# Attention block with two layer norms: the bias add of the layer-norm stages moves from VectorE to GpSimd

## The chip, the cores and the metric

One Trainium2 chip, all 8 cores running the same program, each on two of the 16 sequences. The metric is the device time of the slowest core in microseconds (us). Below, PE is TensorE, DVE is VectorE, ACT is ScalarE, POOL is GpSimd and SP is SyncE.

## What is computed

Layer 0 of a transformer with post layer norms; x is 16 x 2048 x 1024 in float32.

```python
x = _layernorm(x + attn(x, W_attn, b_attn, W_proj, b_proj))      # 16 heads of 64, causal
x = _layernorm(x + ffn(x, G1_R, G2_R, G1_I, G2_I, b_real, b_imag))

# attn ends with:            y @ W_proj + b_proj
# ffn, halves of the row being real and imaginary part:
out_real = x_real @ W_real.T - x_imag @ W_imag.T + bias_real
out_imag = x_real @ W_imag.T + x_imag @ W_real.T + bias_imag
```

The FFN is one product with a 1024 x 1024 matrix built from W_real and W_imag. So each half of the layer ends alike: a 1024 x 1024 product, plus a bias, plus the residual, then a layer norm over the 1024 columns (no gain, no shift).

## The kernel before

A scheduler class (`Sched`) collects the instructions of each engine in five lists, in the order in which `S.emit(engine, ...)` is called; "pe", "ac", "dv", "po" and "sy" are PE, ACT, DVE, POOL and SP. Each engine runs its list strictly in that order. Waits are semaphore counts: ("dv", v) means that DVE must have completed its v-th counted instruction. POOL's list holds DMA issues as well as arithmetic.

Per sequence (`s_i` is 0, 1) the stages are: load x in 16 tiles of 128 tokens and transpose them on PE (`emit_xload`, `emit_xtp`, `emit_xevac`); the V product; attention by pairs of heads, with the Q and K products of the next pair mixed in; a reload of x into `x_tok` (16 tiles side by side, 128 x 1024 float32 each) by four DMAs issued on POOL (line 713); and then two calls of `linear_ln`:

- the first call (`x1_mode` true, called LN1 here) multiplies the attention output by `Wp_sb`, adds the bias `bp_bc` and `x_tok`, normalises, and leaves the result in `x_tok` (float32) and, transposed by PE, in `yfeat` (bf16);
- the second (LN2) multiplies `yfeat` by `Wbig_sb`, adds `bf_bc` and `x_tok`, normalises in place and stores the rows.

In `linear_ln`, for tile `tt`:

- `stage_a(tt)`: PE does 16 matmuls into `ps_s[tt % 2]`, one of two PSUM buffers, each of which comes free when `t2` has read it. Then `t2a` (line 751) adds the bias row, spread over 128 partitions in bf16, to the tile of `x_tok`. `t2` (line 758) adds the matmul result out of PSUM. `st1`, `st2` (lines 763, 767) and `ag` (line 771) form mean and variance, on DVE. `l1` and `l2` (lines 777, 781) on ACT turn the variance into 1/sqrt by Ln and Exp.
- `stage_b1`, kept as `stageB[tt]`: `nm` (line 787, DVE) forms -mean/sqrt(var). In LN1, `xb` (line 792, ACT) writes the normalised tile in bf16 to `x1stage`, and `xf32` (line 801, POOL) then normalises `x_tok` in place, waiting for `xb`. In LN2 `xf32` (line 809, POOL) waits for `nm`, and SP stores the tile (line 815).
- `stage_b2(tt)`, LN1 only: PE transposes `x1stage` (line 826), ACT copies the result to `yfeat` (line 846).

The order in which the tiles are put into the lists is written in this loop:

```python
            for tt in range(n_tt):
                if x1_mode and tt > 2:
                    stage_b2(tt - 3)
                if tt > 0:
                    stageB[tt - 1]()
                stageB[tt] = stage_a(tt)
```

`n_tt` is 16. With two sequences and two calls `t2a` is emitted 64 times.

Of the kernel before, what the change touches and what calls it, by code (L numbers as in the profile page):

```python
# [51 lines left out]
def build(n_seq=2, n_tt=16):  # L52
# [78 lines left out]
    S = Sched()  # L131
# [25 lines left out]
    def bias_bcast(dst, wait_qb, src_row=None):  # L157
# [4 lines left out]
        for jh in range(2):  # L162
# [7 lines left out]
            def cp(v, jh=jh, dst=dst):  # L170
# [7 lines left out]
                  inc="q_b", amt=16)  # L178
# [3 lines left out]
                  waits=[("q_b", S.val("q_b")), ("pe", v_pe_bv)],  # L182
                  inc="q_b", amt=16)
    v_bpbc, v_pe_bp = bias_bcast(bp_bc, v_qb)
    S.emit("po", lambda g: g.dma_start(out=row_bf[0:1, 0:512], in_=b_real[:]),
           waits=[("q_b", S.val("q_b")), ("pe", v_pe_bp)], inc="q_b", amt=16)
    v_qb = S.emit("po", lambda g: g.dma_start(out=row_bf[0:1, 512:1024],
                                              in_=b_imag[:]),
                  waits=[("q_b", S.val("q_b"))], inc="q_b", amt=16)
# [14 lines left out]
    for fi, wdst in enumerate([w2r_d, w2i_d]):  # L204
        vpe = 0
        for m in range(8):
# [10 lines left out]
            vpe = S.emit("pe", mm, waits=w_list, inc="pe" if m == 7 else None)  # L217
# [6 lines left out]
        for m in range(8):  # L224
            sem = "q_w2" if m % 2 == 0 else "q_w3"
            ring = "sy"
            def stf(g, m=m, fi=fi, wdst=wdst):
# [4 lines left out]
                   inc=sem, amt=16)  # L232
# [4 lines left out]
    for wave in range(2):  # L237
# [3 lines left out]
        for i in range(4):  # L241
# [4 lines left out]
                waits=w_extra, inc="q_wa", amt=16)  # L246
        v_wa_ld = S.val("q_wa")
        for i in range(4):
            cc = wave * 4 + i
            if i % 2 == 0:  # L250
# [3 lines left out]
                    waits=[("q_wa", v_wa_ld)], inc="ac")  # L254
            else:
# [3 lines left out]
                    waits=[("q_wa", v_wa_ld)], inc="dv")  # L259
# [7 lines left out]
        inc="q_bt", amt=16)  # L267
# [7 lines left out]
                   waits=[("q_m", v_id)], inc="dv")  # L275
    v_bqkbf = emit_qm(lambda s: s.dma_start(out=bqk_bf[:], in_=battn_d[:],
                                            transpose=True),
                      waits=[("q_bt", v_battn)])
# [3 lines left out]
                   waits=[("q_m", v_bqkbf)], inc="ac")  # L282
# [32 lines left out]
    for dc in range(CC):  # L315
# [3 lines left out]
            inc="q_w", amt=16)  # L319
# [5 lines left out]
    for s_i in range(n_seq):  # L325
# [5 lines left out]
        def sbc(name, shape, dtype):  # L331
# [9 lines left out]
            waits=[G["x_tok"], G["v_all"], ("ac", v_wa_ac), ("dv", v_wa_dv),  # L341
                   ("pe", v_setup_pe)],
            inc="dv")
# [163 lines left out]
        for hp in range(NPAIR):  # L507
# [170 lines left out]
            def yst_store(s, s_i=s_i, hp=hp, yst_=ystage[par]):  # L678
# [4 lines left out]
                         inc="q_ys%d" % par, amt=16)  # L683
            G["yst%d" % par] = ("q_ys%d" % par, vys)
            ys_val.append(vys)
            if hp >= 6:
                v_xf_free = S.val("pe")
                for hp2 in (range(7) if hp == 6 else [7]):
# [5 lines left out]
                           waits=[("q_ys%d" % (hp2 % 2), ys_val[hp2]),  # L694
                                  ("pe", v_xf_free)],
                           inc="q_yf", amt=16)
# [10 lines left out]
        for q4 in range(n_tt // ntq):  # L707
            def xt(s, s_i=s_i, q4=q4, ntq=ntq, x_tok=x_tok):
# [9 lines left out]
                   inc="q_xt", amt=16)  # L718
        v_xt = S.val("q_xt")

        def linear_ln(win_sb, w_wait, feat_ready_fn, bias_bc, v_bias, x1_mode,
# [3 lines left out]
            def stage_a(tt):  # L725
                feat_ready = feat_ready_fn(tt)
                reg = ps_s[tt % 2]
                vpe = 0
                for dc in range(CC):
                    for jh in range(2):  # L730
# [8 lines left out]
                        if dc == 0 and jh == 0:  # L739
                            w_list.append(G["ps_s%d" % (tt % 2)])  # L740
                        r = S.emit("pe", mm, waits=w_list,
                                   inc="pe" if (dc == CC - 1 and jh == 1) else None)
                        if r:
                            vpe = r
# [4 lines left out]
                def t2a(v, tt=tt, x_tok=x_tok, bias_bc=bias_bc):  # L749
                    xt_ = x_tok[:, tt * 1024:(tt + 1) * 1024]  # L750
                    return v.tensor_tensor(xt_, xt_, bias_bc[:], ALU.add)  # L751
                v_t2a = S.emit("dv", t2a,
                               waits=[("q_xt", v_xt), ("dv", v_bbc),
                                      ("po", v_po_base), G["x_tok"]],
                               inc="dv")
                def t2(v, tt=tt, par=par, x_tok=x_tok, reg=reg):
                    xt_ = x_tok[:, tt * 1024:(tt + 1) * 1024]
                    return v.tensor_tensor(xt_, xt_, reg, ALU.add)  # L758
                v_t2 = S.emit("dv", t2, waits=[("pe", vpe), ("dv", v_t2a)],
                              inc="dv")  # L760
                G["ps_s%d" % par] = ("dv", v_t2)
                def st1(v, tt=tt, x_tok=x_tok, stt=stt):
# [7 lines left out]
                def ag(v, mv=mv, stt=stt):  # L770
                    return v.bn_aggr(mv[:, 0:2], stt[:])  # L771
                vag = S.emit("dv", ag,
                             waits=[("dv", vs2), ("ac", ln_guard[sl]["ac"]),
                                    ("dv", ln_guard[sl]["dv"]),
                                    ("po", ln_guard[sl].get("po", 0))], inc="dv")
# [73 lines left out]
# [6 lines that stand above are left out]
# [88 lines left out]
```

How the kernel before makes its waits and increments, by code:

```python
    def run(self, eng_name, engine, sems):  # L40
        floors = {}
        for waits, fn, inc, amt in self.ops[eng_name]:
            for s, v in waits:
                if v and v > floors.get(s, 0):
                    engine.wait_ge(sems[s], v)
                    floors[s] = v
            instr = fn(engine)
            if inc is not None:
                instr.then_inc(sems[inc], amt)
# [850 lines left out]
            @block.sync  # L900
            def _(s):
                S.run("sy", s, sems)
                s.wait_ge(sems["q_out"], v_out_final)
```

## Time and profile before

| | |
|---|---|
| time, median of 3 runs | 1643.38 us (1639.96 to 1705.62) |
| profiled execution: time / span of its slowest core (core 6) | 1641.53 / 1640.0 us |
| spans of the 8 cores | 1617.6 to 1640.0 us |
| busy PE / DVE / ACT / POOL | 1099.8 / 579.2 / 704.6 / 139.8 us |
| DVE `t2a`, both biases | 64 times, 77.8 us |
| POOL `xf32`, LN1 / LN2 | 38.2 / 63.2 us, 32 times each |

Times within the profile are microseconds from the start of the span. A busy share is an average over stages that differ; the timeline lists the instructions of all engines by their start, and is the view in which an order of waits can be followed. Where the rows below are of the timeline, each begins with start and duration, and the brackets at its end give the idle time of that engine before it and what ended that. Runs of like instructions are merged (x16), their duration being that from the first to the last.

### The profile page before, as it was taken

What the parts mean: (1) busy time and instruction counts of PE and PEld (TensorE: products, weight loads), DVE (VectorE), ACT (ScalarE), POOL (GpSimd) and SP (SyncE); (2) the same over time, 40 slices, a digit from 0 to 9 for tenths busy, and PEclk for the clock granted to TensorE, in tenths of its full rate; (3) what the DMA queues carried; (4) which work ended last, traced back from release to release, by engine and by line L of the source; (5) the groups of instructions that cost most, each with busy time, mean ns of one, the idle gap of its engine ahead of it and who ended that gap; (6) DMA issues with size and microseconds to landing.
All of it is one profiled execution on the core that took longest, in us unless ns stands there. A gap on an engine that the chain in (4) does not pass through costs nothing.

```text
span 1640.0 us, 23234 instructions; the slowest of 8 cores (1617.6 to 1640.0 us)
## 1 busy us (share of the span) xinstructions
PE 1099.8 (67%) x8742; PEld 533.6 (33%) x8742; DVE 579.2 (35%) x1075; ACT 704.6 (43%) x842; POOL 139.8 (9%) x137
## 2 busy tenths in 40 slices
PE   2179677677667765476757966767766777467764
PEld 1145233333333332133324523333333333223321
DVE  1245221221222221276774522122222212147676
ACT  1100175567567566054110026746755666414311
POOL 2010100000000000022331000000000000002133
PEclk9999898998999897798998999889999988779898
DMA  7865100000000033600225100000000004340022
GB/s 197 207 115 73 34 2 14 14 1 14 14 21 1 20 63 68 211 1 1 90 103 163 56 1 8 7 14 14 1 14 14 1 14 91 93 152 1 13 95 98
DMA packets 116532, 86.58 MB, mean 53 GB/s; under 512 B 101440, under 2 KB 101576, under 8 KB 115400
## 3 DMA queue, kind: packets, MB, share of 16 engines
q1 hardware_dynamic: 104024, 34.65, 9.7%
q0 software_dynamic: 10912, 37.76, 7.7%
q10 hardware_dynamic: 1488, 12.69, 2.4%
q8 instruction: 73, 1.20, 0.3%
q14 instruction: 35, 0.29, 0.1%
HBM read 52.59 MB, written 26.22 MB: 48 GB/s over the span
## 4 chain that ended last, share of the span: by engine, by line
PE 34%; DVE 21%; ACT 16%; DMA 14%; issue 13%; DVEq 1%; POOL 0%; ACTq 0%; POOLq 0%; SPq 0%
PE ps_g L468 15%; ACT p L554 14%; PE ps_big L535 7%; PE ps_y L606 7%; DVE x_tok L758 5%; DMA w2r_d<-w2big 5%; DVE x_tok L751 5%; DMA x_tok<-x_in 4%; PE ps_big L407 3%; DMA w2i_d<-w2big 3%; DVE stats_sb L763 3%; DVE kp L483 3%; DVE stats_sb L767 2%; ACT mv_sb L777 1%; ACT mv_sb L781 1%
## 5 line engine op out<-in xcount | busy, mean ns | idle before, releaser
L554 ACT ACTIVATE p<-ps_big,consts 128x1024 bf16<-128x1024 f32 (+3 forms) x640 | 586.3, 989 | 516.7 <-PE ps_big L535 514.2
L535 PE MATMUL ps_big<-qp,kp 64*128 64x512 bf16 (+3 forms) x1280 | 226.4, 378 | 172.9 <-ACT p L554 155.7
L468 PE MATMUL ps_g<-x_feat,W_sb 128*128 128x512 bf16 x1024 | 279.0, 405 | 47.4 <-DVE kp L483 35.5
L570 DVE TENSOR_TENSOR pd<-p,mask_sb 128x256 bf16<-128x256 bf16 x256 | 74.5, 291 | 451.8 <-ACT p L554 377.7
L606 PE MATMUL ps_y<-v_all,p 128*128 128x65 bf16 x3840 | 196.6, 204 | 18.4 <-ACT p L554 18.4
L606 PEld LDWEIGHTS ps_y<-v_all,p 128*128 128x128 bf16 x3840 | 153.1, 104 | 96.0 <-issue 91.1
L535 PEld LDWEIGHTS ps_big<-qp,kp 64*128 64x128 bf16 x1280 | 66.7, 94 | 329.2 <-issue 316.8
L733 PE MATMUL ps_big<-Wp_sb,x_feat 128*128 128x512 bf16 x512 | 123.4, 398 | 67.4 <-DMA x_feat<-ystage_d 45.8
L777 ACT ACTIVATE mv_sb<-mv_sb,consts 128x1 f32<-128x1 f32 x64 | 18.8, 294 | 320.9 <-DVE mv_sb L771 320.9
L733 PE MATMUL ps_big<-Wbig_sb,x_feat 128*128 128x512 bf16 x512 | 119.8, 391 | 41.2 <-DVE x_tok L758 41.2
L468 PEld LDWEIGHTS ps_g<-x_feat,W_sb 128*128 128x128 bf16 x1024 | 91.2, 103 | 153.1 <-issue 90.8
L407 PE MATMUL ps_big<-W_sb,x_feat 128*128 128x512 bf16 x512 | 116.4, 383 | 0.0
L483 DVE TENSOR_SCALAR qp<-ps_g,bqk 128x512 bf16<-128x512 f32 x64 | 47.7, 746 | 180.9 <-PE ps_g L468 176.7
L733 PEld LDWEIGHTS ps_big<-Wp_sb,x_feat 128*128 128x128 bf16 x512 | 49.9, 101 | 131.7 <-issue 82.8
L606 PE MATMUL ps_y<-v_all,pd 128*128 128x65 bf16 x512 | 60.7, 202 | 42.6 <-DVE rwave L640 25.4
L733 PEld LDWEIGHTS ps_big<-Wbig_sb,x_feat 128*128 128x128 bf16 x512 | 49.3, 100 | 110.9 <-issue 59.7
L758 DVE TENSOR_TENSOR x_tok<-x_tok,ps_big 128x1024 f32<-128x1024 f32 x64 | 78.1, 1221 | 15.6 <-PE ps_big L733 9.1
L483 DVE TENSOR_SCALAR kp<-ps_g,bqk 128x512 bf16<-128x512 f32 x64 | 47.8, 747 | 82.0 <-PE ps_g L468 82.0
L809 POOL TENSOR_SCALAR x_tok<-x_tok,mv_sb 128x1024 f32<-128x1024 f32 x32 | 63.2, 1975 | 119.2 <-DVE mv_sb L787 119.2
L370 PE MATMUL ps_y<-idf_sb,xstage 128*128 128x128 f32 x192 | 30.1, 301 | 62.4 <-DMA idf_sb<-ident 40.0
L407 PEld LDWEIGHTS ps_big<-W_sb,x_feat 128*128 128x128 bf16 x512 | 50.5, 99 | 55.9 <-issue 2.1
L751 DVE TENSOR_TENSOR x_tok<-x_tok,bp_bc 128x1024 f32<-128x1024 f32 x32 | 38.9, 1216 | 74.3 <-DMA x_tok<-x_in 74.3
(58 smaller groups left out, 647.7 us busy)
## 6 DMA issues: line engine op xcount, KB each, us to landing
xstage<-x_in POOLq DMA_DIRECT2D x32, 512.0 KB, 5.4
x_tok<-x_in POOLq DMA_DIRECT2D x8, 2048.0 KB, 22.6
out<-x_tok SPq DMA_DIRECT2D x32, 512.0 KB, 2.6
wstage<-w_attn ACTq DMA_DIRECT2D x8, 1536.0 KB, 15.7
ystage_d<-yst SPq DMA_DIRECT2D x16, 512.0 KB, 3.8
Wp_sb<-w_proj POOLq DMA_DIRECT2D x8, 256.0 KB, 10.6
Wbig_sb<-w2r_d POOLq DMA_DIRECT2D x8, 128.0 KB, 2.5
w2r_d<-w2big SPq DMA_DIRECT2D x8, 64.0 KB
```

The lines of the kernel that those rows point to most:

```text
L407: return t.matmul(reg[:, jh * 512:(jh + 1) * 512], x_feat[:, cc * T + tt * 128:cc * T + (tt + 1) * 128], W_sb[:, cc * 3072 + 2048 + jh * 5 ...
L468: return t.matmul(ps_g[:], W_sb[:, cc * 3072 + j0:cc * 3072 + j0 + 128], x_feat[:, cc * T + tg * 512:cc * T + (tg + 1) * 512], start=(cc = ...
L483: return v.tensor_scalar(dstbuf[:, tg * 512:(tg + 1) * 512], ps_g[:], bqk[:, bcol:bcol + 1], None, ALU.add)
L535: return t.matmul(ps_big[:, off:off + ln], kpb[e * 64:(e + 1) * 64, kk * 128:(kk + 1) * 128], qpb[e * 64:(e + 1) * 64, pos:pos + ln], star ...
L554: return a.activation(o, i, AF.Exp, bias=consts[:, 0:1], scale=0.125)
L570: return v.tensor_tensor(po_, pp, mm_, ALU.mult)
L606: return t.matmul(ps_y[b_][:, off:off + 65], lhs_ap, v_all[:, vcol:vcol + 65], start=first, stop=is_bank_last)
L733: return t.matmul(reg[:, jh * 512:(jh + 1) * 512], yfeat[:, dc * T + tt * 128:dc * T + (tt + 1) * 128], win_sb[:, dc * 1024 + jh * 512:dc ...
L751: return v.tensor_tensor(xt_, xt_, bias_bc[:], ALU.add)
L758: return v.tensor_tensor(xt_, xt_, reg, ALU.add)
L763: return v.bn_stats(stt[:, 0:6], x_tok[:, tt * 1024:tt * 1024 + 512])
L809: return g.tensor_scalar(x_tok[:, tt * 1024:(tt + 1) * 1024], x_tok[:, tt * 1024:(tt + 1) * 1024], mv[:, 2:3], mv[:, 3:4], ALU.mult, ALU.add)
```

## The change

`t2a` is emitted on POOL and not on DVE: the same addition over the same tile, with its completion counted on POOL's semaphore. `t2` waits for that count. The place of the call in the program is unchanged, so in POOL's list `t2a(tt)` stands where the loop above puts it.

```diff
-                v_t2a = S.emit("dv", t2a,
+                v_t2a = S.emit("po", t2a,
                                waits=[("q_xt", v_xt), ("dv", v_bbc),
                                       ("po", v_po_base), G["x_tok"]],
-                               inc="dv")
+                               inc="po")
                 def t2(v, tt=tt, par=par, x_tok=x_tok, reg=reg):
                     xt_ = x_tok[:, tt * 1024:(tt + 1) * 1024]
                     return v.tensor_tensor(xt_, xt_, reg, ALU.add)
-                v_t2 = S.emit("dv", t2, waits=[("pe", vpe), ("dv", v_t2a)],
+                v_t2 = S.emit("dv", t2, waits=[("pe", vpe), ("po", v_t2a)],
                               inc="dv")
```

## Rows read from the trace of the kernel before

**Rows 1.** Busy us by stretch: PE, PEld, DVE, ACT, POOL; granted clock, DMA share, GB/s

```profile
700.00:740.00 40.00, 31.34 (x182) 14.65 (x182) 31.05 (x46) 19.29 (x29) 9.56 (x8) 1.00 0.00 1
```

**Rows 2.** Timeline (start us, us, engine, line): first and last t2, LN1; last, LN2

```profile
684.64 1.22 DVE L758 TENSOR_TENSOR x_tok<-x_tok,ps_big 128x1024 f32<-128x1024 f32 x1
...
764.19 1.22 DVE L758 TENSOR_TENSOR x_tok<-x_tok,ps_big 128x1024 f32<-128x1024 f32 x1
...
857.07 1.22 DVE L758 TENSOR_TENSOR x_tok<-x_tok,ps_big 128x1024 f32<-128x1024 f32 x1
```

**Rows 3.** Timeline, sequence 1, LN1: one tile in the middle of the stage

```profile
716.30 1.22 DVE L758 TENSOR_TENSOR x_tok<-x_tok,ps_big 128x1024 f32<-128x1024 f32 x1
...
717.62 0.70 DVE L763 BATCH_NORM_STATS2 stats_sb<-x_tok 128x6 f32<-128x512 f32 x1
...
718.23 0.68 DVE L767 BATCH_NORM_STATS2 stats_sb<-x_tok 128x6 f32<-128x512 f32 x1
719.08 0.21 DVE L771 BATCH_NORM_AGGREGATE mv_sb<-stats_sb 128x2 f32<-128x12 f32 x1 [0.17 <-DVE stats_sb L767]
719.38 0.29 ACT L777 ACTIVATE mv_sb<-mv_sb,consts 128x1 f32<-128x1 f32 x1 [2.60 <-DVE mv_sb L771]
719.77 0.29 ACT L781 ACTIVATE mv_sb<-mv_sb,consts 128x1 f32<-128x1 f32 x1
719.97 0.99 ACT L846 COPY x_feat<-ps_y 128x1024 bf16<-128x1024 bf16 x1
720.17 0.21 DVE L787 TENSOR_SCALAR mv_sb<-mv_sb 128x1 f32<-128x1 f32 x1 [0.88 <-ACT mv_sb L781]
720.30 1.21 DVE L751 TENSOR_TENSOR x_tok<-x_tok,bp_bc 128x1024 f32<-128x1024 f32 x1
720.86 1.24 ACT L792 ACTIVATE x1stage<-x_tok,mv_sb 128x1024 bf16<-128x1024 f32 x1
721.62 1.22 DVE L758 TENSOR_TENSOR x_tok<-x_tok,ps_big 128x1024 f32<-128x1024 f32 x1
...
722.27 1.20 POOL L801 TENSOR_SCALAR x_tok<-x_tok,mv_sb 128x1024 f32<-128x1024 f32 x1 [4.13 <-ACT x1stage L792]
```

**Rows 4.** Timeline, sequence 1, LN2: Exp of one tile to t2 of the next

```profile
807.34 0.29 ACT L781 ACTIVATE mv_sb<-mv_sb,consts 128x1 f32<-128x1 f32 x1
807.74 0.21 DVE L787 TENSOR_SCALAR mv_sb<-mv_sb 128x1 f32<-128x1 f32 x1 [0.88 <-ACT mv_sb L781]
807.87 1.22 DVE L751 TENSOR_TENSOR x_tok<-x_tok,bf_bc 128x1024 f32<-128x1024 f32 x1
808.12 2.03 POOL L809 TENSOR_SCALAR x_tok<-x_tok,mv_sb 128x1024 f32<-128x1024 f32 x1 [3.29 <-DVE mv_sb L787]
809.19 1.22 DVE L758 TENSOR_TENSOR x_tok<-x_tok,ps_big 128x1024 f32<-128x1024 f32 x1
```

**Rows 5.** Timeline, sequence 1: the last tile of LN2 and POOL's next instruction

```profile
860.95 0.21 DVE L787 TENSOR_SCALAR mv_sb<-mv_sb 128x1 f32<-128x1 f32 x1 [0.88 <-ACT mv_sb L781]
861.33 1.19 POOL L809 TENSOR_SCALAR x_tok<-x_tok,mv_sb 128x1024 f32<-128x1024 f32 x1 [3.29 <-DVE mv_sb L787]
862.47 1.65 POOL L358 DMA_DIRECT2D xstage<-x_in  x3
```

**Rows 6.** Timeline, sequence 1: the passage from LN1 to LN2

```profile
770.17 1.19 POOL L801 TENSOR_SCALAR x_tok<-x_tok,mv_sb 128x1024 f32<-128x1024 f32 x1 [4.13 <-ACT x1stage L792]
...
770.95 13.30 PE L733 MATMUL ps_big<-Wbig_sb,x_feat 128*128 128x512 bf16 x49
...
771.47 1.23 DVE L751 TENSOR_TENSOR x_tok<-x_tok,bf_bc 128x1024 f32<-128x1024 f32 x1 [3.19 <-POOL x_tok L801]
...
777.25 1.22 DVE L758 TENSOR_TENSOR x_tok<-x_tok,ps_big 128x1024 f32<-128x1024 f32 x1 [4.56 <-PE ps_big L733]
```

**Rows 7.** All instructions of line 809, duration ns min/median/max

```profile
L809 POOL TENSOR_SCALAR x_tok<-x_tok,mv_sb x32: 1194/2027/2035, 781.4 to 1632.8; 128x1024 f32<-128x1024 f32 x32
```

**Rows 8.** Timeline, POOL at the start

```profile
0.49 0.10 POOL L58 MEMSET const-float32-0.0<- 128x1 f32 x1 [0.49 <-issue]
```

## Prediction, made before the changed kernel ran

> **What bounds the kernel now.** I read the instructions grouped by line first. The edited instruction, the bias add (t2a, line 751), runs 64 times on DVE (VectorE), 32 in each of two stages: the projection with its layer norm (call it LN1) and the feed-forward product with its own (LN2). So only these two stages matter, and there the busy table by stretch says that no engine is full: DVE has 31 of 40 us, PE 31 of 40 at the full granted clock of 1.00, ACT 19, POOL 10 [rows 1]. A stage in which nobody is full and every tile takes the same time is a loop of waits, and that must be read in order of time.
>
> The tiles are regular. In LN1 the add of the matmul result (t2, line 758) of tile 0 starts at 684.64 and that of tile 15 at 764.19: 15 intervals of 5.30 us. In LN2 the same from 777.25 to 857.07: 15 of 5.32 [rows 2, 6]. The four stages of the program (two sequences) hold 60 such intervals.
>
> What closes the loop is seen in one tile of LN1 [rows 3]: t2 16.30, statistics 17.62 and 18.23, their aggregate 19.08, then over to ACT for Ln 19.38 and Exp 19.77, back to DVE for the small product nm 20.17, t2a of the next tile 20.30, t2 of the next tile 21.62 (minutes of the clock left out: all are 700 and so much). That is 5.32 us, all DVE except the 1.09 us from the aggregate's start to nm's. PE is not in it: its result for t2 was there before. Nor are the ACT scaling xb (20.86) and the POOL scaling xf32 (22.27): they hang beside the loop. In LN2 it is the same loop with xf32 started straight from nm [rows 4].
>
> **The change part by part.** *Removed.* t2a leaves DVE. From its start to t2's is 1.32 us (20.30 to 21.62) in LN1 and the same in LN2 (807.87 to 809.19). Had nothing else changed, an interval would be 4.00 us.
>
> *Added and moved.* t2a goes into POOL's program, and POOL takes its instructions in written order. The loop over tiles calls the second half of tile k first (it emits xf32 of k on POOL) and then the first half of tile k+1 (t2a of k+1 on POOL). So on POOL t2a(k+1) stands behind xf32(k), and xf32(k) waits for ACT's xb(k) in LN1 or DVE's nm(k) in LN2, both of which need the statistics of tile k, and so t2(k). Then t2(k+1) waits for t2a(k+1). The add, which needs nothing but the input, is thereby tied behind the whole normalisation of the tile before. Everything queued behind it waits too: the statistics of k+1 on DVE, and through the PSUM buffer that t2 frees, the matmuls of k+3. The loop now runs DVE, ACT, POOL, DVE in series.
>
> *Interval in LN1* from start to start [rows 3]: t2 to first statistics 1.32, to the second 0.61, to the aggregate 0.85, to Ln 0.30, to Exp 0.39. From Exp to xb 1.09: between them ACT runs the copy of transposed data of tile k-2 (19.97, 0.99 us), which the program puts before xb; its data will be ready early, but its place in ACT's order stays. From xb's start to xf32's 1.41 (20.86 to 22.27), xf32 itself 1.20. Sum 7.17. Then t2a of duration D. POOL adds no gap before it: at the end of LN2 its next instruction, a DMA issue, starts at 862.47 while xf32 ends at 862.52 [rows 5]. POOL's end to DVE's start is 0.11 (771.36 to 771.47) [rows 6]. So the interval is 7.28 + D.
>
> *Interval in LN2*: the same 3.47 up to Exp, Exp to nm 0.40 [rows 4], nm to xf32 0.38 and xf32 1.19 [rows 5], then D and 0.11: 5.55 + D. Here I take xf32 at 1.19 and not at its median 2.03 [rows 7]. The long ones start while DVE runs t2a, a two-input add out of SBUF (807.87 to 809.09), and end at 810.15, 1.06 after it; the last tile has no t2a beside it and takes 1.19. In the changed loop DVE is idle while POOL works, so the stretch by 0.84 goes away. The Trainium skill has this as a rule (SBUF — State Buffer, section "SBUF: two separate sides"): GpSimd and a DVE instruction with two SBUF inputs exclude each other for a whole instruction. By that rule, with which these rows agree, 1.19 is the value to use too.
>
> *The unknown D.* No two-input POOL instruction is in the trace. The one-input one over the same 1024 columns takes 1.19, which is the low end (D = 1.19: the second input is free). A memset of one column takes 0.10 [rows 8], so 1.09 of the 1.19 goes with the columns; if two inputs are fetched one after the other, D = 0.10 + 2 x 1.09 = 2.28. I take that, since a one-input instruction shows a whole column pass for one fetch and one store. The high end adds half a pass for the bf16 bias, whose conversion no POOL row shows: 2.83.
> The Trainium skill (GPSIMD Engine Reference, section "Elementwise — side-by-side cycle accounting") speaks against this change: its two-input add takes 1.96 times DVE's time. From the 1.22 of this trace, an estimate by that page is 2.38, and the sum below would come out about 6 us higher.
>
> *Sum* with D = 2.28. LN1: 9.56 against 5.32, 4.24 x 30 = 127 us. LN2: 7.83 against 5.32, 2.51 x 30 = 75 us. The first tile of each sequence: t2a on POOL in front of t2, 2.28 + 0.11 for 1.32, twice 1.07 = 2 us. The passage from LN1 to LN2, twice: t2a starts at about 771.4 on POOL and ends at 773.7, while t2 waits for PE until 777.25 [rows 6], so nothing. The tail after the last t2: nothing. Together 204 us.
>
> *Priced at nothing, and what covers it.* PE's matmuls: those of tile k+2 start when t2(k) ends, and have until t2(k+2), over 14 us. Even the 16 right after a pause of PE, slower than those of a busy stretch, were done 6.3 us after their start (770.95 to 777.25) [rows 6], so a granted clock that falls since PE idles more stays hidden. Without that cover 6.3 us would stand in each interval. The stores of output are issued one per tile and have more time than now. The loads of the second sequence's input stand on POOL behind the last xf32, as before; that point just comes later, and is in the sum.
>
> The profiled execution has a span of 1640.0 us and a time of 1641.5; the median of the runs is 1643.4. I add to the median: 1643.4 + 204 = 1847. In the span it reads 1844.
>
> **The rivals.**
> *The add runs ahead on POOL (ends on the other side).* If t2a(k+1) were out of the way before xf32(k), the interval would fall to 4.00, and PE's own 31.34 of 40 us, or 4.17 a tile in LN1 [rows 1], would be next. Gain 30 x 1.15 + 30 x 1.32 = 74 us: 1569. It decides as soon as POOL need not finish xf32(k) first; POOL's time, 1.19 + 2.28 a tile, would fit into 4.00. For it speaks that the add's inputs are loaded long before; against it the written order, which even D = 0 doesn't get round: then LN1 is 7.28 and LN2 5.55, both over 5.32, and the time 1643 + 59 + 7 - 2 = 1707, still slower. A free add does not rescue the change.
> *A cheap POOL add.* The order binds but the second input is nearly free, D = 1.19: LN1 8.47, LN2 6.74, 30 x 3.15 + 30 x 1.42 = 137 us, 1780. For it: I have no row of the instruction.
> *xf32 in LN2 stays at 2.03.* If its length comes from something other than DVE's t2a, the output stores for instance, 30 x 0.84 = 25 us more: 1872. Against it: the last tile's 1.19 under running stores.
> *High D.* 2.83 gives 62 x 0.55 = 34 us more: 1881.
>
> **How the numbers follow.** The loop through POOL with D from 1.7 to 2.83 and xf32 at 1.19: 8.2 in 10, which is the forecast, 1847. Cheap add (down to 1780) 0.5 in 10, xf32 at 2.03 0.5 in 10, the add running ahead 0.3 in 10; 0.2 in 10 that part of it is hidden so that the time stays within 2%, and 0.3 in 10 for something dearer than 1885. The range takes in both bounds of D: 1780 to 1885. Two per cent, about what a measurement of this kernel can tell from no change, is 33 us; every case with the order bound lies above that. Faster 0.03, same 0.02, slower 0.95.
>
> **What would show it.** In the changed profile: intervals between starts of t2 of about 9.6 in LN1 and 7.8 in LN2; POOL busy share up by 64 x 2.28 = 146 less some 25 us for shorter xf32; a POOL add that begins where xf32 ends; DVE's t2 and PE's matmuls with long idle time before them, released by POOL and by t2. The ordering step is wrong if t2a starts before the preceding xf32 has run. The D step is wrong if the POOL add is not near 2.3. The contention step is wrong if xf32 of LN2 is still at 2.03. The sum is wrong if anything outside the two stages moves by more than a few us.

## The result: slower by 11 per cent

| | before | after |
|---|---|---|
| median of all runs | 1644.42 us (8 runs) | 1829.77 us (8 runs, 1828.77 to 1832.77) |
| ratio, 95% interval | | 1.114 [1.1124, 1.1156] |
| span of the profiled core | 1640.0 us | 1828.0 us |
| mean granted clock, slowest core | 0.905 | 0.872 |

The forecast was 1847 in a range of 1780 to 1885, slower with 0.95. Against the median of 1643.4 that it started from, 186 us were added where 204 were forecast. Some executions of every kernel here run at a lower granted clock on one die or both and take some per cent longer; the ratios leave the clear cases out, and where a run below has no ratio its time is that of its fastest execution.

The top of the page of the kernel after (busy us by engine):

```profile
PE 1159.5 (63%) x8742; PEld 548.8 (30%) x8742; DVE 506.2 (28%) x1011; ACT 705.1 (39%) x842; POOL 248.5 (14%) x201
```

POOL is busy 109 us more, DVE 73 us less, and the span is 188 us longer: no engine's load accounts for that. The time goes into waiting. The instructions of one tile in LN1 of the kernel after, in order of time, up to the next tile's t2, with two sets of matmuls beside it (columns as in [rows 3]):

```profile
734.94 1.22 DVE L758 TENSOR_TENSOR x_tok<-x_tok,ps_big 128x1024 f32<-128x1024 f32 x1 [5.28 <-POOL x_tok L751]
736.27 0.69 DVE L763 BATCH_NORM_STATS2 stats_sb<-x_tok 128x6 f32<-128x512 f32 x1
...
736.31 3.61 PE L733 MATMUL ps_big<-Wp_sb,x_feat 128*128 128x512 bf16 x16 [3.55 <-DVE x_tok L758]
736.88 0.68 DVE L767 BATCH_NORM_STATS2 stats_sb<-x_tok 128x6 f32<-128x512 f32 x1
737.65 0.21 DVE L771 BATCH_NORM_AGGREGATE mv_sb<-stats_sb 128x2 f32<-128x12 f32 x1
737.96 0.30 ACT L777 ACTIVATE mv_sb<-mv_sb,consts 128x1 f32<-128x1 f32 x1 [6.58 <-DVE mv_sb L771]
738.35 0.29 ACT L781 ACTIVATE mv_sb<-mv_sb,consts 128x1 f32<-128x1 f32 x1
738.55 0.99 ACT L846 COPY x_feat<-ps_g 128x1024 bf16<-128x1024 bf16 x1
738.75 0.21 DVE L787 TENSOR_SCALAR mv_sb<-mv_sb 128x1 f32<-128x1 f32 x1 [0.88 <-ACT mv_sb L781]
739.44 1.24 ACT L792 ACTIVATE x1stage<-x_tok,mv_sb 128x1024 bf16<-128x1024 f32 x1
...
740.86 1.20 POOL L801 TENSOR_SCALAR x_tok<-x_tok,mv_sb 128x1024 f32<-128x1024 f32 x1 [6.02 <-ACT x1stage L792]
742.02 2.12 POOL L751 TENSOR_TENSOR x_tok<-x_tok,bp_bc 128x1024 f32<-128x1024 f32 x1
744.24 1.22 DVE L758 TENSOR_TENSOR x_tok<-x_tok,ps_big 128x1024 f32<-128x1024 f32 x1 [5.28 <-POOL x_tok L751]
...
745.60 6.57 PE L733 MATMUL ps_big<-Wp_sb,x_feat 128*128 128x512 bf16 x16 [4.17 <-DVE x_tok L758]
```

From t2 to t2 9.30 us, where [rows 3] had 5.32. Each instruction begins about when its predecessor in the chain is done, and the chain runs over DVE, ACT and POOL in series. (What xb at 739.44 stands behind is ACT's copy for an earlier tile, 738.55 + 0.99, and not nm, which was done at 738.96.) The two POOL rows are the point: the add (742.02, line 751) comes at the very end of xf32 of the tile before (740.86 + 1.20), though its inputs have been in place since the stage's first add. DVE's t2 then had 5.28 us of idle time, ended by POOL. The same in LN2, from t2 to t2 with the statistics left out:

```profile
847.32 1.22 DVE L758 TENSOR_TENSOR x_tok<-x_tok,ps_big 128x1024 f32<-128x1024 f32 x1 [3.56 <-POOL x_tok L751]
...
851.12 0.21 DVE L787 TENSOR_SCALAR mv_sb<-mv_sb 128x1 f32<-128x1 f32 x1 [0.88 <-ACT mv_sb L781]
851.51 1.20 POOL L809 TENSOR_SCALAR x_tok<-x_tok,mv_sb 128x1024 f32<-128x1024 f32 x1 [4.30 <-DVE mv_sb L787]
852.67 2.12 POOL L751 TENSOR_TENSOR x_tok<-x_tok,bf_bc 128x1024 f32<-128x1024 f32 x1
854.90 1.22 DVE L758 TENSOR_TENSOR x_tok<-x_tok,ps_big 128x1024 f32<-128x1024 f32 x1 [3.56 <-POOL x_tok L751]
```

The interval is 7.58 us, against 5.32. (7.58 and 9.30 are the regular values. In most stages one or two intervals are about 0.3 longer, in the kernel before as well; there ACT stood idle for 0.37 us between Ln and Exp, and no run says why.) xf32 (line 809) takes 1.20 here and not the 2.03 of [rows 4]; all 32 of them do (duration ns min/median/max, to be held against [rows 7]):

```profile
L809 POOL TENSOR_SCALAR x_tok<-x_tok,mv_sb x32: 1194/1196/1199, 843.9 to 1820.9; 128x1024 f32<-128x1024 f32 x32
```

Who the 64 t2 of the kernel after waited for (us, times): 60 waited for POOL's add, four for PE. Of the four two are at the passages from LN1 to LN2, and the other two stand in regular intervals of 7.58.

```profile
L758 DVE TENSOR_TENSOR x_tok<-x_tok,ps_big x64: 1220/1221/1222, 689.2 to 1816.4; 128x1024 f32<-128x1024 f32 x64
...
  POOL x_tok L751: 339.3, 60
  PE ps_big L733: 23.3, 4
```

At the passage from LN1 to LN2 the add is hidden as forecast: it ends at 837.63 and PE's first result is what t2 waits for, as in [rows 6].

```profile
828.25 1.22 DVE L758 TENSOR_TENSOR x_tok<-x_tok,ps_big 128x1024 f32<-128x1024 f32 x1 [5.28 <-POOL x_tok L751]
...
834.94 7.42 PE L733 MATMUL ps_big<-Wbig_sb,x_feat 128*128 128x512 bf16 x29
...
835.51 2.12 POOL L751 TENSOR_TENSOR x_tok<-x_tok,bf_bc 128x1024 f32<-128x1024 f32 x1
...
839.73 1.22 DVE L758 TENSOR_TENSOR x_tok<-x_tok,ps_big 128x1024 f32<-128x1024 f32 x1 [7.46 <-PE ps_big L733]
```

Last, the granted clock. In [rows 1] it was 1.00 over a stretch of LN1. After, with PE idle longer in each tile, it is 0.79 in a stretch of LN1 (same columns):

```profile
700.00:820.00 120.00, 75.13 (x311) 31.30 (x309) 37.37 (x65) 33.36 (x51) 42.64 (x26) 0.79 0.00 0
```

A full set of 16 matmuls took 3.61 us at the high level (736.31, granted clock 1.00, 2.4 GHz) and 6.57 where the clock had fallen (745.60, granted clock 0.54, most of it at 1.2 GHz). Both intervals around them are 9.30 long: in the regular tiles this cost nothing.

### The profile page after: what moved, and what is told of

Its sections match the earlier page's. It is cut to its first block, busy times and chain, and to the rows that moved or that the text cites. A ratio compares the mean times of both kernels' runs of the same rounds, so it can differ in the third digit from the quotient of the medians.

```text
span 1828.0 us, 23183 instructions; the slowest of 8 cores (1810.0 to 1828.0 us)
## 1 busy us (share of the span) xinstructions
PE 1159.5 (63%) x8742; PEld 548.8 (30%) x8742; DVE 506.2 (28%) x1011; ACT 705.1 (39%) x842; POOL 248.5 (14%) x201
## 4 chain that ended last, share of the span: by engine, by line
PE 31%; ACT 17%; DVE 15%; issue 13%; DMA 12%; POOL 11%; DVEq 1%; ACTq 0%; POOLq 0%; SPq 0%
PE ps_g L468 13%; ACT p L554 12%; POOL x_tok L751 7%; PE ps_big L535 6%; PE ps_y L606 6%; DVE x_tok L758 4%; DMA w2r_d<-w2big 4%; DMA x_tok<-x_in 4%; PE ps_big L407 3%; DMA w2i_d<-w2big 3%; DVE kp L483 2%; DVE stats_sb L763 2%; ACT x1stage L792 2%; DVE stats_sb L767 2%; POOL x_tok L801 2%
## 5 line engine op out<-in xcount | busy, mean ns | idle before, releaser
L733 PE MATMUL ps_big<-Wp_sb,x_feat 128*128 128x512 bf16 x512 | 164.3, 493 | 158.3 <-DVE x_tok L758 108.7
L733 PE MATMUL ps_big<-Wbig_sb,x_feat 128*128 128x512 bf16 x512 | 146.8, 453 | 73.4 <-DVE x_tok L758 73.4
L733 PEld LDWEIGHTS ps_big<-Wp_sb,x_feat 128*128 128x128 bf16 x512 | 59.6, 120 | 253.9 <-issue 228.8
L733 PEld LDWEIGHTS ps_big<-Wbig_sb,x_feat 128*128 128x128 bf16 x512 | 55.8, 112 | 163.6 <-issue 128.4
L713 POOL DMA_DIRECT2D x_tok<-x_in x8 | 5.9, 746 | 557.6 <-DMA ystage_d<-yst 557.6
L751 POOL TENSOR_TENSOR x_tok<-x_tok,bp_bc 128x1024 f32<-128x1024 f32 x32 | 67.8, 2119 | 63.1 <-DMA x_tok<-x_in 63.1
L751 POOL TENSOR_TENSOR x_tok<-x_tok,bf_bc 128x1024 f32<-128x1024 f32 x32 | 67.9, 2121 | 0.3
```

Source lines behind the costliest of these rows:

```text
L733: return t.matmul(reg[:, jh * 512:(jh + 1) * 512], yfeat[:, dc * T + tt * 128:dc * T + (tt + 1) * 128], win_sb[:, dc * 1024 + jh * 512:dc ...
```

## The experiments

Two theories were put against each other. **Order**: the add stands behind the normalisation of the previous tile in POOL's list, and this closes a chain through all engines. **Length**: POOL takes 2.12 us where DVE takes 1.22, or the two engines hinder each other. Intervals below are from t2 to t2, from the profile. Each edit is given against the changed kernel unless said otherwise, with lines left out marked by `...`; `add_bias(tt)` holds the function `t2a` and its `S.emit` on POOL, both taken out of `stage_a` as they were.

### The same work, another order on POOL (e1_order)

```diff
             for tt in range(n_tt):
                 ...
+                v_t2a = add_bias(tt)
                 if tt > 0:
                     stageB[tt - 1]()
-                stageB[tt] = stage_a(tt)
+                stageB[tt] = stage_a(tt, v_t2a)
```

> The add stays on POOL, but t2a of tile k+1 is put into POOL's list ahead of xf32 of tile k, and so only behind xf32 of tile k-1. Theory (the written order closes the loop): the chain of 9.30 us in LN1 and 7.58 in LN2 now spans two tiles, 4.65 and 3.79 a tile; DVE without the add needs 4.00. So the interval is 4.65 in LN1 and 4.0 in LN2, against 5.32 before: about 30 x 0.67 + 30 x 1.32 = 60 us faster than before, 1585. Rival (POOL's slower add is the cause, or POOL and DVE get in each other's way): no faster than before, in the extreme about 1830 as with the change.

Measured: 1583.27 us, ratio to the kernel before 0.9635 [0.9619, 0.965]. That is 246 us less than the changed kernel, by the same instructions on the same engines; one call has moved. In LN2 the interval is 3.98, the 4.00 that the prediction had for the loop of DVE and ACT without the add. In LN1 it averages 4.61 and alternates, mostly between 3.98 and 5.32 in the first sequence and between 4.34 and 4.96 in the second, in pairs that sum to 9.30: the length of the changed kernel's chain, now over two tiles. POOL's xf32 and add, and DVE's t2, in order of time in LN1:

```profile
712.81 1.20 POOL L803 TENSOR_SCALAR x_tok<-x_tok,mv_sb 128x1024 f32<-128x1024 f32 x1 [2.03 <-ACT x1stage L794]
...
713.97 2.13 POOL L728 TENSOR_TENSOR x_tok<-x_tok,bp_bc 128x1024 f32<-128x1024 f32 x1
...
716.20 1.22 DVE L760 TENSOR_TENSOR x_tok<-x_tok,ps_big 128x1024 f32<-128x1024 f32 x1 [1.30 <-POOL x_tok L728]
...
717.95 2.12 POOL L728 TENSOR_TENSOR x_tok<-x_tok,bp_bc 128x1024 f32<-128x1024 f32 x1
...
720.18 1.22 DVE L760 TENSOR_TENSOR x_tok<-x_tok,ps_big 128x1024 f32<-128x1024 f32 x1
...
725.50 1.22 DVE L760 TENSOR_TENSOR x_tok<-x_tok,ps_big 128x1024 f32<-128x1024 f32 x1 [1.30 <-POOL x_tok L728]
```

At 716.20 and 725.50 t2 waits for an add that waited for xf32; the t2 between, at 720.18, doesn't wait. The length theory is out: this kernel's adds are as long, 2.12 to 2.13, and DVE's t2 beside them is still 1.22.

### One tile more of lead (e4_lead1)

```diff
+            biased = [add_bias(tt) for tt in range(1)]
             for tt in range(n_tt):
+                if tt + 1 < n_tt:
+                    biased.append(add_bias(tt + 1))
                 ...
                 if tt > 0:
                     stageB[tt - 1]()
-                stageB[tt] = stage_a(tt)
+                stageB[tt] = stage_a(tt, biased[tt])
```

> As with the add put ahead of the preceding xf32, but one tile further ahead still: t2a of tile k+2 stands in front of xf32 of tile k. Theory: the chain through POOL now spans three tiles, 3.1 us a tile in LN1, and is off the path; LN1 falls from 4.65 to what PE needs (31.34 of 40 us of the kernel before, 4.2 a tile), LN2 stays at DVE's 4.00. About 1573, some 12 us below the version with one tile less of lead. Rival (LN1 was bound by DVE at 4.0 or by PE at once, not by the two-tile chain): the same time as with one tile less.

Measured: ratio 0.9587 [0.9532, 0.9642]; the four executions behind it took 1565.3 to 1581.5 us, the profiled one 1566.1. This interval overlaps that of e1_order, so that the gain over it rests on the profile: LN1 falls to 4.00, all intervals 3.98 but for a few. So the two-tile chain was indeed what held LN1 at 4.61, and with three tiles it is off the path. What holds LN1 at 3.98 now is the loop of DVE and ACT:

```profile
717.92 1.22 DVE L760 TENSOR_TENSOR x_tok<-x_tok,ps_big 128x1024 f32<-128x1024 f32 x1
...
720.63 0.21 DVE L773 BATCH_NORM_AGGREGATE mv_sb<-stats_sb 128x2 f32<-128x12 f32 x1
720.94 0.29 ACT L779 ACTIVATE mv_sb<-mv_sb,consts 128x1 f32<-128x1 f32 x1 [1.26 <-DVE mv_sb L773]
721.33 0.29 ACT L783 ACTIVATE mv_sb<-mv_sb,consts 128x1 f32<-128x1 f32 x1
721.73 0.21 DVE L789 TENSOR_SCALAR mv_sb<-mv_sb 128x1 f32<-128x1 f32 x1 [0.88 <-ACT mv_sb L783]
721.90 1.22 DVE L760 TENSOR_TENSOR x_tok<-x_tok,ps_big 128x1024 f32<-128x1024 f32 x1
```

t2 follows nm without a wait, and of the 64 t2 the view of who ended the idle time before them lists one for PE, at the passage to LN2 (us, times):

```profile
  PE ps_big L742: 7.6, 1
```

PE is close behind. The same stretch as in [rows 1], with ten tiles in it and not seven and a half, and, in the other sequence, two sets of matmuls that begin 3.90 us apart:

```profile
700.00:740.00 40.00, 39.74 (x243) 19.99 (x247) 28.75 (x51) 26.28 (x40) 32.75 (x21) 1.00 0.00 1
...
1436.83 3.62 PE L742 MATMUL ps_big<-Wp_sb,x_feat 128*128 128x512 bf16 x15
...
1440.73 3.62 PE L742 MATMUL ps_big<-Wp_sb,x_feat 128*128 128x512 bf16 x16
```

So the expected 4.2 for PE was too high: PE can do a tile of LN1, transposes and all, in 3.90. Its busy time in [rows 1] counts the ends of pipelined matmuls, each recorded at 0.38 us where the next starts 0.22 after it. For the same reason 39.74 us busy of 40 doesn't show PE to be what binds.

### An almost free add in the old place (e3_short_add)

```diff
-                    xt_ = x_tok[:, tt * 1024:(tt + 1) * 1024]
-                    return v.tensor_tensor(xt_, xt_, bias_bc[:], ALU.add)
+                    xt_ = x_tok[:, tt * 1024:tt * 1024 + 1]
+                    return v.tensor_tensor(xt_, xt_, bias_bc[:, 0:1], ALU.add)
```

> The add on POOL takes one column only and not 1024 (the bias of the other columns is left out), its place in the list is unchanged. Theory: order binds even with an almost free add: LN1 9.30 - 2.0 = 7.3, LN2 7.58 - 2.0 = 5.6, so 1644 + 30 x 2.0 + 30 x 0.25 = about 1707, slower than before. Rival (the length of the POOL add is the cost): with the add gone from DVE and nearly free on POOL the interval falls to 4.0 to 4.3 and the time to about 1570.

This kernel leaves out the bias of 1023 of the 1024 columns. Measured: 1712.6 us, intervals 7.36 in LN1 and 5.65 in LN2. With the work of the add practically gone from both engines, the kernel is still 70 us slower than the one that did it on DVE. Its xf32, the add of one column and t2:

```profile
734.58 1.20 POOL L801 TENSOR_SCALAR x_tok<-x_tok,mv_sb 128x1024 f32<-128x1024 f32 x1 [6.01 <-ACT x1stage L792]
...
735.74 0.19 POOL L751 TENSOR_TENSOR x_tok<-x_tok,bp_bc 128x1 f32<-128x1 f32 x1
...
736.03 1.22 DVE L758 TENSOR_TENSOR x_tok<-x_tok,ps_big 128x1024 f32<-128x1024 f32 x1 [3.35 <-POOL x_tok L751]
```

The add shrank by 1.93 us (2.12 to 0.19), and so did both intervals (9.30 to 7.36, 7.58 to 5.65). That is what being on the chain means: one to one.

### One stage at a time (e2_ln1_only, e2_ln2_only)

```diff
-                v_t2a = S.emit("po", t2a,
+                t2a_on = "po" if x1_mode else "dv"       # e2_ln2_only: "not x1_mode"
+                v_t2a = S.emit(t2a_on, t2a,
                 ...
-                v_t2 = S.emit("dv", t2, waits=[("pe", vpe), ("po", v_t2a)],
+                v_t2 = S.emit("dv", t2, waits=[("pe", vpe), (t2a_on, v_t2a)],
```

> The add is on POOL in LN1 and back on DVE in LN2. Theory: the two stages add up. LN1 keeps its 9.30 us interval (8.92 for the first two), LN2 goes back to 5.32: 1644 + 2 x 59 = about 1762. In LN2 xf32 is again 2.03 us where a DVE add runs beside it. If the stages are not independent the time lies elsewhere, and if xf32's 2.03 comes from something other than the DVE add it stays at 1.20.

Measured: 1762.42 us, ratio 1.0727 [1.0704, 1.075]; 9.29 in LN1, 5.32 in LN2, 119 us over the kernel before.

> The add is on POOL in LN2 and back on DVE in LN1. Theory: the part of LN2 alone, 30 x (7.58 - 5.32) = 68 us, 1712; together with the 118 us of LN1 alone the 186 us of the whole change. If a share of the loss came from both at once, the two parts don't add up.

Measured: 1706.3 us, about 64 over the kernel before; the other of its two executions, the profiled one, took 1720.8, and the ratio over both is 1.0425 [1.0347, 1.0504]. The intervals are 5.32 and 7.58. With 1706.3 the parts sum to 183 of the 186 us, and each stage shows the same interval as where both are changed: the stages are independent. The first kernel also has xf32 of LN2 beside a DVE add once more, and its mean is again that of long ones (line 810 is line 809 moved by the edit; busy us, mean ns, idle before):

```profile
L810 POOL TENSOR_SCALAR x_tok<-x_tok,mv_sb 128x1024 f32<-128x1024 f32 x32 | 63.2, 1975 | 117.7 <-DVE mv_sb L788 117.7
```

### What stretched xf32 beside the add (e6_one_input)

```diff
                 def t2a(v, tt=tt, x_tok=x_tok, bias_bc=bias_bc):
                     xt_ = x_tok[:, tt * 1024:(tt + 1) * 1024]
+                    if not x1_mode:
+                        return v.tensor_copy(xt_, xt_)
                     return v.tensor_tensor(xt_, xt_, bias_bc[:], ALU.add)
```

This is the kernel before with that one edit, on DVE; it leaves the bias of LN2 out.

> The kernel before, with DVE's t2a in LN2 replaced by a copy of the tile onto itself: one input out of SBUF instead of two (the bias of the second product is left out). It asks what stretches POOL's xf32 from 1.20 to 2.03 beside it. If only a two-input DVE instruction holds POOL up, xf32 takes 1.20. If any DVE instruction that uses both ports does, the copy too holds it up, for as long as the copy lasts: the stretch then equals what is left of the copy when xf32 comes. The copy itself is expected at 0.6 us, half of the add, which shortens the interval by 0.6 to 4.7.

Measured: 1627.4 us, interval 4.79, the copy 0.68 us, xf32 1.49:

```profile
806.09 0.21 DVE L789 TENSOR_SCALAR mv_sb<-mv_sb 128x1 f32<-128x1 f32 x1 [0.88 <-ACT mv_sb L783]
806.22 0.68 DVE L752 COPY x_tok<-x_tok 128x1024 f32<-128x1024 f32 x1
806.48 1.49 POOL L811 TENSOR_SCALAR x_tok<-x_tok,mv_sb 128x1024 f32<-128x1024 f32 x1 [3.29 <-DVE mv_sb L789]
807.01 1.22 DVE L760 TENSOR_TENSOR x_tok<-x_tok,ps_big 128x1024 f32<-128x1024 f32 x1
```

So a one-input DVE instruction out of SBUF can hold POOL up as well. xf32 ends 1.07 us after the copy's end (807.97 less 806.90); beside the add of [rows 4] it ended 1.06 after the add's. In both cases it does almost all its work once DVE is through, whatever DVE's length. t2, which runs right after and has an input in PSUM, doesn't slow it. The Trainium skill says the same (SBUF — State Buffer, "SBUF: two separate sides"): of a GpSimd instruction and a DVE instruction that is in a two-port mode, as a float32 copy within SBUF is, or has two SBUF inputs, the one that starts first holds the shared ports for its whole length. The trace agrees: in both rows the DVE instruction had started first, 0.25 to 0.26 us before xf32.

### What sets the length of the POOL add (e7_f32_bias)

```diff
+            v_b32 = S.emit("dv", lambda v: v.tensor_copy(bias32[:], bias_bc[:]), ...)
...
-                    return v.tensor_tensor(xt_, xt_, bias_bc[:], ALU.add)
+                    return v.tensor_tensor(xt_, xt_, bias32[:], ALU.add)
```

> The changed kernel, with the bias spread out in float32 and not in bf16 (one DVE copy of 0.7 us at the start of each stage makes it). It asks what sets the 2.12 us of the POOL add, which was forecast at 2.28. If the columns alone count, the add stays at 2.12, the intervals at 9.30 and 7.58, and the time at 1830. If a float32 second input is dearer, as two passes of the one-input instruction would make it (2.28) or the ratio 1.96 to DVE's add from the Trainium skill (GPSIMD Engine Reference, Elementwise), 2.38, the intervals grow by 0.16 to 0.26 each and the time by 10 to 16 us.

Measured: 1841.8 us, intervals 9.51 and 7.80, and the add at 2.34:

```profile
L757 POOL TENSOR_TENSOR x_tok<-x_tok,bias 128x1024 f32<-128x1024 f32 x64 | 149.7, 2339 | 63.9 <-DMA x_tok<-x_in 61.9 <-DVE bias L725 2.0
```

Against 2.12 with a bf16 bias, the type of the second input counts for 0.22 us. The intervals grew by 0.21 and 0.22, again one to one.

### A version that beats both (e5_lead2_late_nm)

```diff
+            biased = [add_bias(tt) for tt in range(2)]
             for tt in range(n_tt):
+                if tt + 2 < n_tt:
+                    biased.append(add_bias(tt + 2))
                 ...
-                if tt > 0:
+                if x1_mode and tt > 0:
                     stageB[tt - 1]()
-                stageB[tt] = stage_a(tt)
+                stageB[tt] = stage_a(tt, biased[tt])
+                if not x1_mode and tt > 0:
+                    stageB[tt - 1]()
```

> As with the add two tiles ahead, with one tile more of lead, and in LN2 the second half of tile k-1 (nm on DVE, xf32 on POOL) is put behind the first half of tile k, so that DVE does not sit through ACT's Ln and Exp. Theory: in LN2 DVE's time per tile falls from 3.98 to about 3.1 and PE's 16 matmuls (3.6 us in the kernel before) are next: interval 3.6, so 30 x 0.38 = 11 us faster than with the add two tiles ahead, while LN1 stays at 3.98 since a chain of three tiles was already off the path. About 1555. Rival (LN2 is bound by something that the order on DVE doesn't touch): the interval stays at 3.98.

Measured: 1549.07 us, ratio 0.9424 [0.9379, 0.947]. LN1 stays at 4.00, where nm has kept its place and one tile more of lead changes nothing; LN2 falls to 3.45. In LN2 DVE now does nm of the tile before (795.56) right behind the aggregate, before ACT's Ln of this tile has begun, and goes on to t2 without standing still through Ln and Exp:

```profile
795.44 0.21 DVE L773 BATCH_NORM_AGGREGATE mv_sb<-stats_sb 128x2 f32<-128x12 f32 x1
795.56 0.19 DVE L789 TENSOR_SCALAR mv_sb<-mv_sb 128x1 f32<-128x1 f32 x1
795.74 0.29 ACT L779 ACTIVATE mv_sb<-mv_sb,consts 128x1 f32<-128x1 f32 x1 [2.42 <-DVE mv_sb L773]
...
796.18 1.22 DVE L760 TENSOR_TENSOR x_tok<-x_tok,ps_big 128x1024 f32<-128x1024 f32 x1 [0.42 <-POOL x_tok L728]
```

t2's short wait is for the add here and for PE in nearly all other tiles. 48 matmuls of LN2 run through in one piece:

```profile
789.79 10.52 PE L742 MATMUL ps_big<-Wbig_sb,x_feat 128*128 128x512 bf16 x48
```

A single set of 16 takes 3.61 in the kernel after; the two further sets here add (10.52 - 3.61) / 2 = 3.45 each, which is the interval: LN2 has come to TensorE. POOL is not far off, busy for 38.16 us of the 40 from 765 to 805. So the expected mechanism held and the gain was larger than the 11 us expected, since 3.6 was read from the row of a single set, which holds the pipeline's tail. The run changes two things in LN2, the lead and the place of nm, and none separates them.

## Why the prediction was right

**The order step** held. The changed profile shows the add starting where xf32 ends, in all 60 tiles that have an xf32 of their stage before them, and e1_order shows the cause from the other side: with the order mended and nothing else, the loss of 186 us becomes a gain of 60. The prediction's figure for a free add, 1707 with intervals of 7.28 and 5.55, stands beside e3_short_add's 1713 with means of 7.34 and 5.67: its add of one column still takes 0.19.

**The interval in LN1**, forecast 9.56, is 9.30. Term by term: D 2.12 and not 2.28, -0.16. From the second statistics to the aggregate 0.77 and not 0.85, -0.08. From xf32's start to the add's 1.16 and not 1.20, -0.04. Every other term agrees to 0.01.

**The interval in LN2**, forecast 7.83, is 7.58, by the same three.

**D**, the one unknown, was bounded by 1.19 and 2.83 and taken at 2.28, two passes of the one-input instruction. It measured 2.12, which is 10 of the 18 us below, and for the same reason POOL is busy 109 us more and not the 121 forecast. The bf16 bias was put into the upper bound as something that could cost extra. e7_f32_bias shows the opposite sign: bf16 is the cheap case, 2.12, and float32, 2.34, lies near the value taken. That 2.28 lies between the two is no proof of two equal passes: neither run gives it. The Trainium skill's ratio of 1.96 (GPSIMD Engine Reference, "Elementwise — side-by-side cycle accounting") gave 2.38 as an estimate, which fits the float32 case within 0.04; for this kernel's bf16 bias the ratio is 2.12 / 1.22 = 1.74. The rival of a cheap POOL add fell with it.

**The aggregate's 0.08** is in the profile of before, and was not seen: in three of the four stages the first three or four intervals were 5.25 and nearly all others 5.32, which the mean of 5.30 in LN1 hid. From the fifth tile on, and in LN1 of the second sequence from the first, the aggregate's list of waits has a guard on POOL's count that nothing before it on DVE has waited for. The scheduler drops a wait if its engine has already waited for as high a count of the same semaphore, and in the changed kernel t2 has just waited for POOL. The two runs with one stage changed bear this out: from the second statistics to the aggregate it is 0.78 (0.77 between the rounded starts above) in every tile of the stage whose add is on POOL, and 0.85 from the fifth tile on in the stage whose add is on DVE. No run took out the wait alone.

**The first two intervals of LN1** are 8.92: the copy of transposed data that delays xb exists only from the third tile on, 0.38 us less in four intervals. The sum over 30 intervals a stage had not taken that out.

**Sum.** 30 x (9.56 - 9.27) = 9 and 30 x (7.83 - 7.60) = 7, with the means of the four stages; the two passages, 11.5 and 12.8 us against 13.06, give 2 more. That makes 18, where 17 lie between 1847 and 1830.

**The contention step** held: xf32 1.20 in all of LN2. The rival that it would stay at 2.03 is out, and e2_ln1_only brings the long one back with the DVE add.

**The terms at nothing** held. The granted clock did fall, to 0.79 in a stretch of LN1, and the sets of matmuls that it lengthened to 6.57 us stayed within the interval.

**The rival on the other side**, the add running ahead, did not happen with the change, and is what e1_order and e4_lead1 make happen. It was priced at 1569 and the profiled execution of e4_lead1 took 1566. That closeness is in part luck: for LN1 the price rested on a PE bound of 4.17, while PE can do a tile in 3.90 and the interval was 3.98, set by the loop of DVE and ACT that the prediction had at 4.00.

## What to carry to other kernels

Moving work to an idle engine moves it into that engine's queue: before its duration is weighed, look at what it will stand behind, and follow that back to see whether it closes a loop with the instruction that waits for it. If it does, the interval is the length of the whole chain divided by the number of tiles that it spans, and both numbers can be read from the timeline before anything is built. Put work whose inputs are ready early ahead of work whose inputs are late; here that one call was worth 246 us, while the move to POOL in the better order gained 60. And a busy share near 100% for PE isn't yet a bound: ask whether anything waits for it.

## What the runs showed of the hardware

The POOL add over 1024 columns took 2.12 us with a bf16 second input and 2.34 with a float32 one, while DVE's took 1.22 with bf16. Nothing in the trace of before had pointed to that difference.

xf32 was held up by a DVE copy of one SBUF input until its end (1.49 in place of 1.20), and not by t2, whose second input is in PSUM; nor were POOL's adds, 2.12 to 2.13 in e1_order, by t2 or the statistics beside them.

A single set of 16 matmuls shows 3.61 us, but a further set in an unbroken run costs 3.45 (e5_lead2_late_nm, at a granted clock of 1.00): read for a bound, the single one is too long.
